# Edge sort of a graph network: two of six value fields multiplied on GpSimd

## What is computed

```
def reference(x, src, dst, edge_weight, ...):
    # layer 0: every edge carries a softmax-weighted row of its source to its target
    msg = h[src][:, None, :] * attn[src][:, :, None]
    neigh = segment_sum(msg, dst, num_segments=n)
    x = layernorm(x + elu(neigh.reshape(n, -1) @ weight))
    # layer 1: three rounds of
    ef = concatenate([nf[src], nf[dst], traj[:, None]])
    msg = leaky_relu(ef @ We.T + be)
    red = segment_sum(msg, dst)
    h = leaky_relu(concatenate([nf, red]) @ Wn.T + bn)
    return layernorm(x + h)
```

## Time and profile before

| | |
|---|---|
| median of 3 runs | 12787.6 us (12770.79 to 12788.03) |
| the profiled execution, own time | 12745.33 us |
| its span, first to last instruction | 12744.1 us |
| mean granted TensorE clock | 0.795 |
| VectorE busy | 9576.1 us, 75% of the span |
| TensorE busy | 9301.9 us, 73% |
| GpSimd busy | 5465.9 us, 43% |
| granted TensorE clock between 148.2 and 1892 us | 1.00 |

### The profile page before, as it was taken

How to read it: one execution, slowest core, us unless ns; L and a number is a source line. 1 busy time by engine, 2 the same in 40 slices (tenths; PEclk the granted TensorE clock), 3 DMA queues, 4 the chain that set the end, 5 groups by cost and what they waited for, 6 DMA issues and landing times. The chain is left out here.

```text
span 12744.1 us, 516143 instructions
## 1 busy us (share of the span) xinstructions
PE 9301.9 (73%) x178370; PEld 8200.3 (64%) x178370; DVE 9576.1 (75%) x22840; ACT 5107.3 (40%) x15575; POOL 5465.9 (43%) x5851
## 2 busy tenths in 40 slices
PE   7999995466577776677666677766666777666666
PEld 6999982255566665676666666766666567566565
DVE  6999994577788887666777776567777755677777
ACT  7888850033266665453112125421121244212112
POOL 0000005700055555345666653356666433566663
PEclk9999995599855555798777779987777799777777
DMA  1000001288655557596444467864444588544445
GB/s 37 8 8 8 8 8 31 65 276 277 232 164 163 163 163 141 191 308 217 149 148 150 149 126 231 291 199 149 148 149 149 110 268 292 191 149 148 148 148 102
DMA packets 1462824, 1932.74 MB, mean 152 GB/s; under 512 B 243474, under 2 KB 1074852, under 8 KB 1461764
## 3 DMA queue, kind: packets, MB, share of 16 engines
q1 hardware_dynamic: 1213169, 1370.74, 33.0%
q0 software_dynamic: 245760, 546.77, 17.5%
q10 hardware_dynamic: 3184, 6.90, 0.2%
HBM read 1202.74 MB, written 725.45 MB: 151 GB/s over the span
## 5 line engine op out<-in xcount | busy, mean ns | idle before, releaser
L1633 POOL DMA_INDIRECT work<-rows,quad_at x2928 | 3276.8, 1119 | 1921.6 <-issue 970.5
L1473 PE MATMUL bank<-work 128*128 128x64 bf16 x46848 | 2836.5, 223 | 816.9 <-issue 697.5
L1473 PEld LDWEIGHTS bank<-work 128*128 128x128 fp8e4 (+1 forms) x46848 | 2426.4, 119 | 1042.9 <-issue 1009.1
L1658 ACT COPY work<-tabs 128x192 bf16 x2928 | 1033.1, 353 | 4150.5 <-remote 2052.9
L1674 PE MATMUL bank<-work 128*128 128x64 bf16 x35136 | 1975.6, 217 | 825.9 <-issue 737.3
L1674 PEld LDWEIGHTS bank<-work 128*128 128x128 fp8e4 x35136 | 1649.7, 114 | 1034.2 <-issue 976.4
L1442 DVE COPY work<-bank 128x256 f32<-128x256 f32 (+1 forms) x3840 | 1616.6, 424 | 881.3 <-PE bank L1418 760.8
L1418 PE MATMUL bank<-work 128*128 128x64 bf16 x46080 | 2164.4, 196 | 20.0 <-issue 19.7
L1418 PEld LDWEIGHTS bank<-work 128*128 128x128 fp8e4 x46080 | 1956.8, 100 | 24.7 <-issue 23.9
L1389 ACT COPY work<-tabs 128x192 bf16 x3840 | 1275.3, 352 | 1739.1 <-PE bank L1418 1370.8
L1707 DVE TENSOR_TENSOR work<-bank,work 128x512 f32<-128x512 f32 x1464 | 1006.8, 688 | 1249.8 <-remote 906.9
(11 more groups left out here) (335 smaller groups left out, 12626.2 us busy)
## 6 DMA issues: line engine op xcount, KB each, us to landing
work<-hits_g SPq DMA_DIRECT2D x1464, 256.0 KB
rows<-work SPq DMA_DIRECT2D x1440, 256.0 KB, 3.4
work<-hits_s SPq DMA_DIRECT2D x1440, 128.0 KB, 3.3
hits_g<-work SPq DMA_DIRECT2D x976, 128.0 KB
rows<-work SPq DMA_DIRECT2D x480, 260.0 KB
work<-rows,quad_at POOLq DMA_INDIRECT x3904
work<-meta_src SPq DMA_DIRECT2D x480, 128.0 KB
hits_s<-work SPq DMA_DIRECT2D x480, 128.0 KB
```

The lines of the kernel that those rows point to most:

```text
L1473: last = ten.matmul(to[:, 0:D], hits_of(j), piece_of(j), start=j == 0 and k == 0, stop=j == QUAD - 1 and k == 2, skip_group_check=True)
L1633: pool.indirect_dma_start(quads[g // 2 % (GATHERED // 2)][:, half(g)], None, table, bass.IndirectOffsetOnAxis(ap=quad_at[:, g:g + 1], axis ...
L1658: sca.copy(window[q % 8].unsqueeze(1), tabs[:, 1, bass.ds(w, 1), :]).then_inc(s_window, 1)
```

## The change

The product of line 735 is split. VectorE makes fields 0 to 3 and raises `s_values`. GpSimd, which had no work in this stage, makes fields 4 and 5 (1024 values a partition of 3072) in a loop of its own over the 391 lots and raises a new semaphore `s_values_too`. It waits for the lot's `hit_col` (the count that VectorE's line 731 reached) and, as `spread` does, for `s_grid` of the lot three before. TensorE's `grid` waits for both semaphores. Nothing else is touched.

```
+    OF_VECTOR = 4
+    column_known = {}
+    def times_columns(lot, first, end):
+        at, t = lot % 3, tile(lot, 0)
+        spread_values = field[block_of(lot) % 4]["values"][:, t // LOT, first:end, :].rearrange("p f (j i) -> p f j i", i=2)
+        return values[at][:, first:end, :, :, :], over(hit_col[at], 1, end - first), over(spread_values, 3, COLS)
...
             ten.wait_ge(s_values, lot + 1)
+            ten.wait_ge(s_values_too, lot + 1)
...
-            column_ok = chain.did(vec.tensor_tensor(hit_col[at], columns(lane_pairs, COLS), twos(lot, "column", COLS), ALU.is_equal))
+            column_ok = column_known[lot] = chain.did(vec.tensor_tensor(hit_col[at], columns(lane_pairs, COLS),
+                                                                        twos(lot, "column", COLS), ALU.is_equal))
             vec.tensor_tensor(hit_row[at], columns(row_pairs, 2 * P), twos(lot, "row", 2 * P), ALU.is_equal)
             chain.wait(column_ok)
-            vec.tensor_tensor(values[at], over(hit_col[at], 1, FIELDS), over(spread_values, 3, COLS), ALU.mult).then_inc(s_values, 1)
+            vec.tensor_tensor(*times_columns(lot, 0, OF_VECTOR), ALU.mult).then_inc(s_values, 1)
...
+    @block.gpsimd
+    def _(pool):
+        for lot in range(NL):
+            pool.wait_ge(*column_known[lot])
+            at_least(pool, s_grid, lot - 2)
+            pool.tensor_tensor(*times_columns(lot, OF_VECTOR, FIELDS), ALU.mult).then_inc(s_values_too, 1)
```

More of the change, by code:

```diff
@@ L436, in build @@
     s_ranked, s_rank, s_rank_sum, s_place = sort("ranked"), sort("rank_read"), sort("rank_summed"), sort("place")
-    s_values, s_grid, s_read, s_step = sort("values"), sort("grid"), sort("grid_read"), sort("vector_chain")
+    s_values, s_values_too, s_grid, s_read, s_step = sort("values"), sort("values_too"), sort("grid"), sort("grid_read"), sort("vector_chain")
     s_stored = [sort(f"grid_stored{n}") for n in range(2)]
@@ L730, in spread @@
             at, t = lot % 3, tile(lot, 0)
-            column_ok = chain.did(vec.tensor_tensor(hit_col[at], columns(lane_pairs, COLS), twos(lot, "column", COLS), ALU.is_equal))
+            column_ok = column_known[lot] = chain.did(vec.tensor_tensor(hit_col[at], columns(lane_pairs, COLS),
+                                                                        twos(lot, "column", COLS), ALU.is_equal))
             vec.tensor_tensor(hit_row[at], columns(row_pairs, 2 * P), twos(lot, "row", 2 * P), ALU.is_equal)
             chain.wait(column_ok)
-            spread_values = field[block_of(lot) % 4]["values"][:, t // LOT, :, :].rearrange("p f (j i) -> p f j i", i=2)
-            vec.tensor_tensor(values[at], over(hit_col[at], 1, FIELDS), over(spread_values, 3, COLS), ALU.mult).then_inc(s_values, 1)
+            vec.tensor_tensor(*times_columns(lot, 0, OF_VECTOR), ALU.mult).then_inc(s_values, 1)
         def read_grid(b):
```

## The result

The changed kernel takes 13216.9 us (median of 4, 13212.47 to 13222.93) against 12787.8 for the kernel before in the same comparison (a fourth execution is in that median now): ratio 1.0339, 95% interval 1.0321 to 1.0357, so 429 us or 3.4% slower. The forecast was 13360, slower, range 12900 to 14000. The direction and the mechanism came out; the price a lot was set too high.

What follows compares the result with a forecast made beforehand. VectorE was taken to lead in the sort, TensorE close behind. Saving 209 us on VectorE's product and losing 782 us to GpSimd's reads gave +573 us on 12788, rounded to 13360 us; range 12900 to 14000.

Steps and rivals of the forecast that it cites:

- VectorE's product loses a third: Line 735 in the sort: 3072 to 2048 elements saves 0.534 us a lot, 209 us; alone, TensorE would set the time.
- GpSimd's product at 2.81 us: GpSimd's new product of 1024 elements in the sort: 2.81 us, hidden beside TensorE's 4.29 us a lot.
- The one-input row that I extended: GpSimd's line 1898: 527 ns for 128 elements, 854 for 256, extended to 2.81 us for 1024; 5.42 if second input costs equally.
- The common path: VectorE and GpSimd reading SBUF in the sort exclude each other; GpSimd's reads cost VectorE about 2.0 us a lot, +782 us.
- one held row: VectorE's line 1922, held 0.12 us behind GpSimd's line 1898: read as 0.98 ns an element, 0.25 us for 256.
- the bounds of 1.0 and 2.81 us: VectorE's loss a lot: 1.0 us if two bf16 values come in one read, 2.81 if the whole operation holds the path.
- The sign that was set for this step: Line 745 would take 3.2 us against 1.22 for twin line 743, or the loss would spread over 743, 745 and 681.
- TensorE's new wait: TensorE's grid also waits for `s_values_too`: costed at nothing, since GpSimd reads ahead of VectorE's own product and ends before it.
- TensorE's clock: In the sort, 28% idle may lower it; at 0.90 a lot takes 4.77 us, under 5.94, so nothing on average.
- The sum: A sort lot goes from 4.48 to 5.94 us; over 391 lots -209 + 782 = +573 us.
- the faster one: No common path in the sort: GpSimd's work hidden, TensorE sets the stage, 62 to 84 us gained, 12715 us; chance 0.14.
- Cheap reads: GpSimd's reads in the sort cost 1.0 us a lot, +182 us, 12970; or 2.0 us partly beside PSUM work, +386; chance 0.10 for about 1 us.

Runs made afterwards that it cites:

- e3: Changed kernel without GpSimd's loop and TensorE's second wait; VectorE makes four fields, fields 4 and 5 zeroed once before the sort: 11202.4 us against 11294.1 for the kernel before.
- e1: Kernel before with nine rounds of single GpSimd and VectorE operations put in front of the sort; GpSimd's two-input product of 1024 values took 1.90 us alone.
- e8: Changed kernel with GpSimd's two-input product replaced by a one-input product with 1.0 of the column rows: +79 us over the kernel before, ratio 1.0065.
- e2: Changed kernel with GpSimd's product replaced by a memset of the same 1024 values: 11203.0 us against 11294.1 for the kernel before, ratio 0.9919.
- e10: Changed kernel, but GpSimd waits for the end of VectorE's line 745 before starting its product: +269 us over the kernel before, ratio 1.0241.
- e4: Changed kernel, but GpSimd starts a lot's product only after VectorE ends line 681 of the next step: 11657.5 us against 11294.1 for the kernel before, ratio 1.0322.

## Why the forecast was right in kind and too high in size

1. *VectorE's product loses a third.* Right: line 745 unheld is 1216 ns, which saves the 209 us. The floor lay 91 us below the kernel before (e3), a little deeper than the 62 to 84 us that I read from TensorE's waits. One reading was loose: TensorE and VectorE stand at 9 from the second slice to the sixth, not in the first, which also holds the preparation; nothing hangs on it.

2. *GpSimd's product at 2.81 us.* The number appeared in the trace to the digit, and that was luck. The product by itself takes 1.90 us; its 2.81 hold 0.91 of waiting. The one-input row that I extended (2.55 ns a value) was right for its own kind, 2.79 us for 1024 values in e1, but the two-input product isn't slower than that, it is faster. The Trainium skill (GPSIMD Engine Reference, section 3, Performance versus the Vector engine) has 4497 ns for a two-input add of 2048 fp32 values; the estimate of half of it, 2.25 us, is above e1's 1.90 us in bf16.

3. *The common path.* This step carried the sum, and its mechanism holds: whoever comes second waits (in 339 of the 391 lots), and only reads count. The term that was mis-sized is the hold, 2.0 us forecast against 1.70 measured. I had taken 0.25 us for 256 values from one held row, as if it were all reading. At 0.83 ns they need 0.21 us, and the remaining 0.04 would belong to the start. No run had fp32 values, so this isn't shown for that row; but e1 has the same 0.04 for the new product, where VectorE was let through 1.74 us after GpSimd's start and not 1.70. Scaled by eight, that start made 0.3 us a lot, 117 us over 391 lots. A second, smaller part is the 52 lots in which GpSimd read beside PSUM work or small jobs. With the measured hold in each lot the sum would have been -209 + 665 = +456; with those lots it is +436. The two parts, 117 and 20 us, are the whole way from +573 to +436. The truth lay well inside the bounds of 1.0 and 2.81 us. That a bf16 value costs as much as an fp32 value had been assumed, on one held row of fp32, and there was some luck in its coming so near. The sign that was set for this step, line 745 at 3.2 us, came as 2.91.

   The rule of the Trainium skill (SBUF — State Buffer, section "SBUF: two separate sides") that the loser is blocked for the whole instruction isn't what the runs show: in e8 a GpSimd instruction that takes 2.79 us by itself (e1) held VectorE for 0.84. What its part "Who interferes with whom" says of the kinds agrees: a GpSimd operation that only writes held no two-input product (e2), a one-input bf16 operation was held (0.69 to 1.99 us, e1), a reduction was not.

4. *TensorE's new wait.* Right that it costs nothing: no wait of TensorE ended with line 781. But TensorE's idle time isn't where I had put it, before the grid and some 1.5 us a lot. It waited there for 14.4 us in all, and for 266.5 us before the counts of line 567, for line 681 of VectorE's next step, which starts late where line 745 was held:

```profile
L613 PE MATMUL bank<-work 128*128 128x192 bf16 (+2 forms) x18750 | 1205.0, 224 | 14.4 <-DVE work L745 14.4
L567 PE MATMUL bank<-work,tabs 128*98 128x125 bf16 x3125 | 405.8, 248 | 329.6 <-DVE tabs L681 266.5 <-issue 42.4 <-ACT work L520 18.4
```

5. *TensorE's clock.* Right that it isn't the bound: a mean of 0.95 over the sort, at 83% busy.

6. *The sum.* Forecast 5.94 us a lot, measured (2322.0 - 139.5)/390 = 5.60; forecast +573 us, measured +429.

Of the rivals, the faster one needed a loss under 0.53 us a lot; e2 and e3 show that its time was reachable only without GpSimd's reads. "Cheap reads" with GpSimd served at line 720 is what e10 built on purpose, at +269 where the text had +386 with 2.0 us of reads; with 1.70 it gives (1.70 - 0.48 - 0.534) x 391 = +268.

## What to carry to other kernels

Work taken from a full VectorE to an idle GpSimd isn't free when VectorE's stream consists of operations with two SBUF inputs: price it by the values that GpSimd reads, not by how long its instruction lasts. Here a value of a two-input product cost VectorE 1.66 ns of holding and had cost it 0.52 ns to make itself, so moving it lost three times what it gained. Writes on GpSimd (2 fields' worth of memset here) and VectorE's operations with a PSUM input and reductions were free of it, and a GpSimd operation should be released so early that it stands ready when such work begins (e10 against e4, 94 us apart). And before a duration of a waiting instruction is believed, one should ask what is in it: twins of the same size, like lines 743 and 745, show the waiting.

## What I had not expected of the hardware

- GpSimd's two-input bf16 product is faster than its one-input `tensor_scalar` on the same 1024 values: 1.90 against 2.79 us.
- A VectorE operation with a single SBUF input (bf16 `tensor_scalar`, 2048 values) is held just as one with two is: 0.69 us alone, 1.99 behind GpSimd's product. Small once-a-block jobs such as line 704 (0.28 to 1.73 us) are held in the same way.
- The order of turns isn't fixed: in 52 of 391 lots of the changed kernel VectorE went on through two more operations while GpSimd waited, and its instruction grew from 2.81 to 4.42 us (3.95 in one). What decides it stays open.
